# A graph layer on one core: source rows by four partitions and a shuffle, TensorE warmed up, tile 0 ahead of the weights

## The chip, the cores and the metric

The kernel runs on one NeuronCore of a Trainium2 chip. The metric is the device time of one execution in microseconds. The kernel before takes 806.27 us, the median of three runs (795.36 to 811.41).

## What is computed

Every edge takes the normalised rows of its two nodes, puts a linear layer and a ReLU on them, and the message is added to the source node's row of x. In float32, cut to what matters (the layer's own names are put in):

```python
def setup_inputs(seed=0):
    # x: normal, (50000, 512) float32
    # src: 12500 random nodes; dst: 12500 nodes, skewed to the low ones
    # src, dst sorted together by dst
    ...

def _layernorm(x, axis=-1, eps=1e-05):
    m = jnp.mean(x, axis=axis, keepdims=True)
    v = jnp.var(x, axis=axis, keepdims=True)
    return (x - m) / jnp.sqrt(v + eps)

def reference(x, src, dst, L0_gnn_W, L0_gnn_b):
    h = jnp.maximum(_layernorm(x), 0.0)
    # W: (512, 1024), b: (512,)
    x_ij = jnp.concatenate([h[src], h[dst]], axis=1)
    m_ij = jax.nn.relu(x_ij @ W.T + b)
    return x + jax.ops.segment_sum(m_ij, src, num_segments=50000)
```

## The kernel before

The 12500 edges make 98 tiles of 128 edges, one edge a partition (`TILES`). For each tile t:

- POOL gathers the 128 rows of x of the sources and the 128 of the destinations with two indirect DMAs into one of eight buffers of `xg` (`gather`, line 183; a row is 2 KB, a tile 0.52 MB). From tile 8 on it waits on `centred`: ACT must have read the tile that had the buffer.
- DVE takes the statistics of both sides (line 234, once per side), and the scales 1/std by a reciprocal and one Newton step (lines 248 to 261). ACT gives the root (line 409), centres with ReLU (397) and scales (404).
- PE transposes both sides by a product with the identity (line 487, four per side). ACT copies the result rounded to fp32r, `ht_hi` (388), and DVE takes what rounding lost, `ht_lo` (267). The weights are split in the same way, `w_hi` (ACT, 381) and `w_lo` (DVE, 345).
- PE makes 24 products of 128x512 per tile (lines 503 to 505): high by high, high by low, low by high, for each of eight chunks of 128 inputs.
- DVE adds the bias (275), ACT applies the ReLU and rounds, `m_hi` (416), DVE takes the low part, `m_lo` (306).
- Tiles go in pairs. DVE compares the sources of a pair with the tile's own, `same` (288), and counts earlier edges with the same source (290); PE multiplies `same` with the messages (515 to 521), so that each edge holds the sum over its pair for its source; ACT stores these sums into `ring`, 52 tiles deep (425). Every edge but the first of a source in a pair is sent to a spare row behind `out` (`lanes`, 297 and 301).
- POOL adds the sums to `out` by indirect DMA (`add`, 199), two per pair. A pair's adds wait until those of the pair before have landed (`scattered`).

The comparison needs the pair's 256 sources along the free axis on all 128 partitions. ACT loads them into `src_row`, one of two buffers, with a DMA that broadcasts 1 KB to 128 partitions (`load_row`, 373): 128 KB per pair of tiles, 49 times, issued in ACT's odd steps for tiles s + 1 and s + 2.

SP loads indices, the weights in four parts (149; the second and later ones wait until tile 0's rows have arrived) and the bias, and then copies x to `out` with 125 DMAs of 800 KB (163), at most three in flight (`COPY_AHEAD`). The first add waits for all of them. The order of POOL's program is fixed: gathers of tiles 0 to 55, and then, from tile `FIRST_ADD` = 56 on, up to seven pairs of adds for eight gathers; the add of pair 0 stands behind the gather of tile 56. The sums of tile 52 and later reuse `ring` and wait for the adds of tile t - 52.

The engines run their own programs and meet at semaphores. A step s of PE is: transposes of tile s + 1, products of tile s, and in even steps the sums of the pair s - 2. A step of DVE is: statistics of s + 2, bias of s - 1, aggregates of s + 2, `same_source` of s - 1, scales of s + 2, low parts of s + 1, low message and lanes of s - 1. Step s of ACT: high parts of s + 1, message of s - 1, root and centring of s + 2, sums, row load, scaling of s + 2. A wait of DVE on a source row therefore stands ahead of the low parts of tile s + 1, for which PE's next products wait.

## Time and profile before

| | us |
|---|---|
| median of three runs | 806.27 |
| fastest and slowest run | 795.36, 811.41 |
| the profiled execution | 808.76 |
| its span in the profile | 807.0 |
| PE, DVE, ACT, POOL busy | 724.0, 572.9, 475.8, 364.6 |

One execution was profiled. Busy time of PE includes its pipelined overlap, so the record of one 128x512 product is about 400 ns long while the next starts after some 230. PEclk is the granted TensorE clock as a share of 2.4 GHz. Waits are put down to the semaphore that came last. `Lnnn` is a line of the kernel before, as numbered above.

### The profile page before, as it was taken

How to read it: one execution, taken by the hardware profiler on the slowest of the kernel's cores; microseconds unless marked ns; L12 is line 12 of the kernel's file. 1: busy time of each engine (PE TensorE's matmuls, PEld its weight loads, DVE VectorE, ACT ScalarE, POOL GpSimd, SP SyncE). 2: the span in 40 equal slices, each digit the busy share in tenths (PEclk: the TensorE clock that was granted, in tenths of full speed). 3: DMA queues.
4: the chain of work that ended last, by engine and by line, in shares of the span. 5: the costliest groups of instructions: out<-in, count | busy, mean ns of one | idle time of the engine just before them, and what ended most of it. 6: DMA issues, size and time to landing. Idle time of an engine off the chain costs nothing.

```text
span 807.0 us, 13243 instructions
## 1 busy us (share of the span) xinstructions
PE 724.0 (90%) x3430; PEld 588.0 (73%) x3430; DVE 572.9 (71%) x1874; ACT 475.8 (59%) x892; POOL 364.6 (45%) x304
## 2 busy tenths in 40 slices
PE   1499999967799998999999999999999999999950
PEld 1387877756688677877888888888888888888840
DVE  4476867645676686777887887878878788787720
ACT  4465656544566574756765667656576665666610
POOL 6522323222222322223257766666776677644343
PEclk9799999999999999999999999999999999999995
DMA  7999999999999999999558877878787778765664
GB/s 223 404 348 362 354 361 354 342 349 355 353 360 357 341 349 359 358 340 358 185 121 153 142 137 153 154 139 156 147 140 145 146 153 134 154 90 75 84 73 58
DMA packets 42414, 188.95 MB, mean 234 GB/s; under 512 B 7894, under 2 KB 14166, under 8 KB 40384
## 3 DMA queue, kind: packets, MB, share of 16 engines
q0 software_dynamic: 29792, 77.00, 45.5%
q1 hardware_dynamic: 5552, 105.39, 34.1%
q10 hardware_dynamic: 7056, 6.43, 3.9%
q14 instruction: 12, 0.10, 0.0%
q8 instruction: 2, 0.03, 0.0%
HBM read 163.19 MB, written 128.61 MB: 362 GB/s over the span
## 4 chain that ended last, share of the span: by engine, by line
DMA 37%; PE 22%; issue 12%; POOL 12%; DVE 8%; another core or an unknown queue 5%; ACT 3%; ACTq 0%; DVEq 0%; SPq 0%; POOLq 0%
DMA out<-ring,add_i 21%; DMA src_row<-src_rows 14%; POOL out L199 9%; PE z_ps L503 5%; PE z_ps L504 5%; PE z_ps L505 5%; PE ht_ps L487 3%; POOL xg L183 3%; DVE ht_lo L267 1%; DMA ring<-w_t 1%; DVE stats L234 1%; DVE m_lo L306 1%; DVE zb L275 1%; ACT h L397 1%
## 5 line engine op out<-in xcount | busy, mean ns | idle before, releaser
L503 PE MATMUL z_ps<-w_hi,ht_hi 128*128 128x512 f32 x784 | 322.2, 411 | 2.0 <-issue 2.0
L504 PE MATMUL z_ps<-w_lo,ht_hi 128*128 128x512 f32 x784 | 312.7, 399 | 0.0
L505 PE MATMUL z_ps<-w_hi,ht_lo 128*128 128x512 f32 x784 | 312.5, 399 | 0.0
L183 POOL DMA_INDIRECT xg<-x,src_i x98 | 103.6, 1058 | 300.7 <-ACT h L397 285.7
L388 ACT CAST ht_hi<-ht_ps 128x512 fp32r<-128x512 f32 x196 | 106.7, 590 | 223.4 <-PE ht_ps L487 201.2
L199 POOL DMA_INDIRECT out<-ring,add_i x98 | 157.7, 1609 | 103.5 <-DMA out<-ring,add_i 86.2
L505 PEld LDWEIGHTS z_ps<-w_hi,ht_lo 128*128 128x128 f32 x784 | 148.9, 190 | 36.7
L503 PEld LDWEIGHTS z_ps<-w_hi,ht_hi 128*128 128x128 f32 x784 | 150.0, 191 | 34.4 <-issue 2.4
L504 PEld LDWEIGHTS z_ps<-w_lo,ht_hi 128*128 128x128 f32 x784 | 149.8, 191 | 32.2
L234 DVE BATCH_NORM_STATS2 stats<-xg 128x6 f32<-128x512 f32 x196 | 125.6, 682 | 36.7 <-DMA xg<-x,dst_i 32.3
L487 PE MATMUL ht_ps<-identity,h 128*128 128x128 f32 x784 | 109.4, 284 | 41.9 <-ACT h L404 41.8
L404 ACT ACTIVATE h<-h,rstd 128x512 f32<-128x512 f32 x196 | 131.6, 724 | 20.3 <-DVE rstd L261 15.0
L487 PEld LDWEIGHTS ht_ps<-identity,h 128*128 128x128 f32 x784 | 95.6, 147 | 59.7 <-ACT h L404 32.6
L397 ACT ACTIVATE h<-xg,neg_mean 128x512 f32<-128x512 f32 x196 | 130.2, 716 | 0.0
L267 DVE TENSOR_TENSOR ht_lo<-ht_ps,ht_hi 128x512 fp32r<-128x512 f32 x196 | 126.2, 686 | 0.0
L183 POOL DMA_INDIRECT xg<-x,dst_i x98 | 102.0, 1040 | 29.9 <-issue 29.9
L416 ACT ACTIVATE m_hi<-zb 128x512 fp32r<-128x512 f32 x98 | 62.9, 642 | 46.8 <-DVE zb L275 41.4
L275 DVE TENSOR_TENSOR zb<-z_ps,bias_bc 128x512 f32<-128x512 f32 x98 | 67.7, 691 | 15.4 <-PE z_ps L505 12.4
L306 DVE SCALAR_TENSOR_TENSOR m_lo<-zb,m_hi 128x512 fp32r<-128x512 f32 x98 | 66.8, 682 | 0.1
L288 DVE TENSOR_SCALAR same<-src_row,src_f 128x128 fp32r<-128x128 int32 x98 | 32.6, 332 | 48.1 <-DMA src_row<-src_rows 43.5
L248 DVE RECIPROCAL rough<-std 128x2 f32<-128x2 f32 x98 | 16.0, 164 | 69.0 <-ACT std L409 68.4
L425 ACT COPY ring<-agg_ps 128x512 f32 (+1 forms) x98 | 52.2, 588 | 2.1 <-PE agg_ps L518 2.1
(40 smaller groups left out, 404.4 us busy)
## 6 DMA issues: line engine op xcount, KB each, us to landing
out<-x SPq DMA_DIRECT2D x125, 800.0 KB
src_row<-src_rows ACTq DMA_DIRECT2D x49, 128.0 KB
ring<-w_t SPq DMA_DIRECT2D x4, 512.0 KB, 5.2
xg<-x,src_i POOLq DMA_INDIRECT x98
xg<-x,dst_i POOLq DMA_INDIRECT x98
out<-ring,add_i POOLq DMA_INDIRECT x98
out<-x SPq DMA_DIRECT2D x1, 512.0 KB
bias_bc<-bias SPq DMA_DIRECT2D x1, 256.0 KB
```

Of the source, the lines that this page charges most:

```text
L183: nc.gpsimd.indirect_dma_start(out=xg[:, b, s, :], out_offset=None, in_=x, in_offset=bass.IndirectOffsetOnAxis(ap=nodes[:, t:t + 1], axis= ...
L199: nc.gpsimd.indirect_dma_start(out=out, out_offset=bass.IndirectOffsetOnAxis(ap=add_i[:, t:t + 1], axis=0), in_=ring[:, t % RING, :], in_o ...
L234: nc.vector.bn_stats(stats[:, b, s, :], xg[:, m, s, :]).then_inc(stats_done, 1)
L267: nc.vector.tensor_tensor(ht_lo[:, b, s, :], ht_ps[b][s][:, :], ht_hi[:, b, s, :].bitcast(F32), ALU.subtract).then_inc(lo_ready, 1)
L275: nc.vector.tensor_tensor(zb[:, b, :], z_ps[b][:, :], bias_bc[:, :], ALU.add).then_inc(biased, 1)
L388: nc.scalar.copy(ht_hi[:, b, s, :], ht_ps[b][s][:, :]).then_inc(hi_ready, 1)
L397: nc.scalar.activation(h[:, b, s, :], xg[:, m, s, :], ACT.Relu, bias=neg_mean[:, b, s:s + 1]).then_inc(centred, 1)
L404: nc.scalar.activation(h[:, b, s, :], h[:, b, s, :], ACT.Copy, scale=rstd[:, b, s:s + 1]).then_inc(h_ready, 1)
L487: last = nc.tensor.transpose(ht_ps[b][s][:, k * P:(k + 1) * P], h[:, b, s, k * P:(k + 1) * P], identity[:, :])
L503: nc.tensor.matmul(z_ps[b][:, :], hi, w_hi[:, c, :], start=(c == 0), stop=False)
L504: nc.tensor.matmul(z_ps[b][:, :], hi, w_lo[:, c, :], start=False, stop=False)
L505: last = nc.tensor.matmul(z_ps[b][:, :], lo, w_hi[:, c, :], start=False, stop=(c == K - 1))
```

## The change

- `load_row` writes the pair's 256 sources to four partitions only (0, 32, 64, 96) of `row_lanes`, 4 KB, with four buffers instead of two. It goes out three pairs ahead. POOL clears `row_lanes` once at the start, and ACT's first four loads wait for that. For each even tile DVE spreads each of the four partitions over its 32 with a `stream_shuffle` into `src_row`, now a single buffer, and waits for its own shuffle (`row_spread`).
- `zb` has one buffer instead of two.
- PE runs 60 transposes of the identity, in a loop of 15 times four, before tile 0's.
- SP issues two weight loads, not one, before it waits for tile 0's rows.
- ACT and DVE make the high and low parts of tile 0 right behind its scaling, ahead of the weights' third and later chunks; DVE takes tile 1's statistics later.
- POOL sets its two bounds registers behind the clearing of `row_lanes`; they are registers in both versions.

```diff
@@ -30,9 +30,12 @@
     PAIRS = TILES // 2
     W_LOADS = 4
     W_FIRST = 2
+    WARM = 60
     XS = 8
     RING = 52
     FIRST_ADD = 56
+    ROWS = 4
+    LANES = 32
     COPY_RUNS = 16
     COPY_ROWS = COPY_RUNS * 25
     COPIES = N // COPY_ROWS
@@ -81,14 +84,15 @@
         h = sb("h", [P, 2, SIDES, D], F32)
         ht_hi = sb("ht_hi", [P, 2, SIDES, KD * P], F32R)
         ht_lo = sb("ht_lo", [P, 2, SIDES, KD * P], F32R)
-        src_row = sb("src_row", [P, 2, 2 * P], I32)
+        row_lanes = sb("row_lanes", [P, ROWS, 2 * P], I32)
+        src_row = sb("src_row", [P, 2 * P], I32)
 
 
         same = sb("same", [P, 3, P], F32R)
         found = sb("found", [P, 2 * P], F32)
         count = sb("count", [P, 2], F32)
         move = sb("move", [P, 2], F32)
-        zb = sb("zb", [P, 2, OUT], F32)
+        zb = sb("zb", [P, OUT], F32)
         m_hi = sb("m_hi", [P, 2, OUT], F32R)
         m_lo = sb("m_lo", [P, 2, OUT], F32R)
 
@@ -108,7 +112,9 @@
         eps_made = sem("eps_made")
         spare_made = sem("spare_made")
         x_arrived = [sem(f"x_arrived{b}") for b in range(XS)]
-        row_arrived = [sem(f"row_arrived{b}") for b in range(2)]
+        lanes_made = sem("lanes_made")
+        row_arrived = [sem(f"row_arrived{b}") for b in range(ROWS)]
+        row_spread = sem("row_spread")
         scattered = sem("scattered")
         src_cast = sem("src_cast")
         w_hi_ready = sem("w_hi_ready")
@@ -142,7 +148,7 @@
             sp.dma_start(src_i[:, :], src_cols).then_inc(src_loaded, 16)
             w_chunks = w_t.rearrange("(k p) o -> p k o", p=P)
             for n in range(W_LOADS):
-                if n == 1:
+                if n == 2:
 
                     sp.wait_ge(x_arrived[0], 16 * SIDES)
                 ks = slice(n * K // W_LOADS, (n + 1) * K // W_LOADS)
@@ -170,8 +176,6 @@
 
         @block.gpsimd
         def _(pool):
-            last_node = pool.to_reg(N - 1)
-            last_row = pool.to_reg(N + 2 * P - 1)
 
             def gather(t):
                 b = t % XS
@@ -201,6 +205,9 @@
                         in_=ring[:, t % RING, :], in_offset=None, bounds_check=last_row,
                         compute_op=ALU.add).then_inc(scattered, 16)
 
+            nc.gpsimd.memset(row_lanes[:, :, :], 0).then_inc(lanes_made, 1)
+            last_node = pool.to_reg(N - 1)
+            last_row = pool.to_reg(N + 2 * P - 1)
             nc.gpsimd.iota(spare_i[:, :], pattern=[[P, 2]], base=N, channel_multiplier=1).then_inc(spare_made, 1)
             nc.gpsimd.memset(eps[:, :], EPS).then_inc(eps_made, 1)
             nc.gpsimd.memset(identity[:, :], 0.0).then_inc(consts, 1)
@@ -272,18 +279,21 @@
                 if not isinstance(t, int):
 
                     dve.wait_ge(stats_done, SIDES * (t + 4))
-                nc.vector.tensor_tensor(zb[:, b, :], z_ps[b][:, :], bias_bc[:, :], ALU.add).then_inc(biased, 1)
+                nc.vector.tensor_tensor(zb[:, :], z_ps[b][:, :], bias_bc[:, :], ALU.add).then_inc(biased, 1)
 
             def same_source(t, m):
 
-                b, row_slot = m % 2, m // 2 % 2
-
-                dve.wait_ge(row_arrived[row_slot], 4 * (t - m) + 16 * (m // 4) + 16)
+                b = m % 2
+                if b == 0:
+                    dve.wait_ge(row_arrived[m // 2], 2 * (t - m) + 16)
+                    nc.vector.stream_shuffle(src_row[:, :], row_lanes[:, m // 2, :], [0] * LANES
+                                             ).then_inc(row_spread, 2)
+                    dve.wait_ge(row_spread, t + 2)
                 if not (isinstance(t, int) and t < 2):
                     dve.wait_ge(agg_done, t - 1)
 
                 width = (b + 1) * P
-                row = src_row[:, row_slot, 0:width]
+                row = src_row[:, 0:width]
                 mine = src_f[:, bass.ds(t, 1)]
                 nc.vector.tensor_scalar(same[:, b:2 * b + 1, :].rearrange("p a j -> p (a j)"), row, mine, None,
                                         ALU.is_equal).then_inc(same_ready, 1)
@@ -303,7 +313,7 @@
 
             def message_low(t, b):
                 dve.wait_ge(mhi_ready, t + 1)
-                nc.vector.scalar_tensor_tensor(out=m_lo[:, b, :], in0=zb[:, b, :], scalar=0.0,
+                nc.vector.scalar_tensor_tensor(out=m_lo[:, b, :], in0=zb[:, :], scalar=0.0,
                                                in1=m_hi[:, b, :].bitcast(F32), op0=ALU.max, op1=ALU.subtract
                                                ).then_inc(mlo_ready, 1)
 
@@ -349,10 +359,10 @@
             statistics(0, 0)
             aggregate(0, 0)
             scales(0, 0)
+            low_parts(0, 0)
+            w_low_parts(W_FIRST, KD)
             statistics(1, 1)
             aggregate(1, 1)
-            w_low_parts(W_FIRST, KD)
-            low_parts(0, 0)
             w_low_parts(KD, K)
             scales(1, 1)
             dve.wait_ge(bias_loaded, 16)
@@ -370,8 +380,8 @@
         def _(act):
             def load_row(t, slot):
 
-                act.dma_start(src_row[:, slot, :],
-                              src_rows[0:1, bass.ds(t * P, 2 * P)].to_broadcast([P, 2 * P])
+                act.dma_start(row_lanes[0::LANES, slot, :],
+                              src_rows[0:1, bass.ds(t * P, 2 * P)].to_broadcast([P // LANES, 2 * P])
                               ).then_inc(row_arrived[slot], 16)
 
             def w_high_parts(first, end):
@@ -413,7 +423,7 @@
                 act.wait_ge(biased, t + 1)
                 if not (isinstance(t, int) and t < 2):
                     act.wait_ge(agg_done, t - 1)
-                nc.scalar.activation(m_hi[:, b, :], zb[:, b, :], ACT.Relu).then_inc(mhi_ready, 1)
+                nc.scalar.activation(m_hi[:, b, :], zb[:, :], ACT.Relu).then_inc(mhi_ready, 1)
 
             def store_sums(t, again):
 
@@ -440,15 +450,16 @@
                     centre(s + 2, (m + 2) % XS)
                 if b and has(-3):
                     store_sums(s - 3, again)
-                if b and has(-2) and has(2):
+                if b and has(-3) and has(2 * ROWS - 2):
 
                     act.wait_ge(counted, s - 1)
-                    load_row(s + 1, (m + 1) // 2 % 2)
+                    load_row(s + 2 * ROWS - 3, (m - 3) % XS // 2)
                 if has(2):
                     divide(s + 2, b)
 
-            load_row(0, 0)
-            load_row(2, 1)
+            act.wait_ge(lanes_made, 1)
+            for pair in range(ROWS):
+                load_row(2 * pair, pair)
             act.wait_ge(eps_made, 1)
 
             nc.scalar.activation(warm[:, :], eps[:, :], ACT.Sqrt)
@@ -456,8 +467,8 @@
             deviation(0, 0)
             centre(0, 0)
             divide(0, 0)
+            high_parts(0, 0)
             w_high_parts(W_FIRST, KD)
-            high_parts(0, 0)
             w_high_parts(KD, K)
             deviation(1, 1)
             centre(1, 1)
@@ -533,6 +544,9 @@
                     sums(s - 2)
 
             pe.wait_ge(consts, 4)
+            with pe.Fori(0, WARM // 4):
+                for k in range(KD):
+                    nc.tensor.transpose(ht_ps[1][0][:, k * P:(k + 1) * P], identity[:, :], identity[:, :])
             transposes(0, 0)
             products(0, 0)
             transposes(1, 1)
```

DVE in the main loop, where the source row is compared (the operations of one even tile). Before:

```order
68 L240 BN_AGGR mean_var<-stats 128x2 x2
69 L242 TENSOR_SCALAR neg_mean<-mean_var 128x2
70 L281 REGISTER_ALU
71 L283 REGISTER_ALU
72 L288 ISA
73 L288 TENSOR_SCALAR same<-src_row,src_f 128x128
74 L290 SCALAR_TENSOR_TENSOR found,count<-src_row,src_f,earlier 128x128
```

Now:

```order
69 L247 BN_AGGR mean_var<-stats 128x2 x2
70 L249 TENSOR_SCALAR neg_mean<-mean_var 128x2
71 L288 ISA
72 L289 STREAM_SHUFFLE src_row<-row_lanes 128x256
73 L291 REGISTER_ALU
74 L293 REGISTER_ALU
75 L298 ISA
76 L298 TENSOR_SCALAR same<-src_row,src_f 128x128
77 L300 SCALAR_TENSOR_TENSOR found,count<-src_row,src_f,earlier 128x128
```

The shuffle stands ahead of `same`, and with it everything of the step behind that; row 71 is part of the wait for the load, 75 of the one for the sums.

ACT at the start, from its first instruction on. Before:

```order
1 L373 DMA src_row<-src_rows 128x256 x2
2 L454 ACT_TABLE_LOAD
3 L454 ACTIVATE warm<-eps 128x1
4 L381 CAST w_hi<-ring 128x512 x2
5 L409 ACTIVATE std<-mean_var,eps 128x2
6 L397 ACTIVATE h<-xg,neg_mean 128x512 x2
7 L404 ACTIVATE h<-h,rstd 128x512 x2
8 L381 CAST w_hi<-ring 128x512 x2
9 L388 CAST ht_hi<-ht_ps 128x512 x2
10 L381 CAST w_hi<-ring 128x512 x4
```

Now:

```order
1 L383 DMA row_lanes<-src_rows 4x256 x4
2 L465 ACT_TABLE_LOAD
3 L465 ACTIVATE warm<-eps 128x1
4 L391 CAST w_hi<-ring 128x512 x2
5 L419 ACTIVATE std<-mean_var,eps 128x2
6 L407 ACTIVATE h<-xg,neg_mean 128x512 x2
7 L414 ACTIVATE h<-h,rstd 128x512 x2
8 L398 CAST ht_hi<-ht_ps 128x512 x2
9 L391 CAST w_hi<-ring 128x512 x6
```

Four small row loads stand where two large ones did, and the two high parts of tile 0 (the cast of `ht_ps`) have moved ahead of six of the eight casts of the weights.

PE at the start. Before:

```order
0 L479 UNCONDITIONAL_BRANCH
1 L487 MATMUL ht_ps<-identity,h 128x128 x8
2 L503 MATMUL z_ps<-w_hi,ht_hi 128x512
```

Now:

```order
0 L490 UNCONDITIONAL_BRANCH
1 L547 UNCONDITIONAL_BRANCH
2 L549 MATMUL ht_ps<-identity 128x128 x4
3 L547 REGISTER_ALU
4 L547 COMPARE_AND_BRANCH
5 L498 MATMUL ht_ps<-identity,h 128x128 x8
6 L514 MATMUL z_ps<-w_hi,ht_hi 128x512
```

Rows 1 to 4 are the loop of the identity's transposes, ahead of those of tile 0.

## Rows read from the trace of the kernel before

**Rows 1.** The page: traffic in 40 slices of 20.2 us, and its HBM line
```profile
GB/s 223 404 348 362 354 361 354 342 349 355 353 360 357 341 349 359 358 340 358 185 121 153 142 137 153 154 139 156 147 140 145 146 153 134 154 90 75 84 73 58
...
HBM read 163.19 MB, written 128.61 MB: 362 GB/s over the span
```
**Rows 2.** The view by stretches: start:end, length, busy us (instructions) of each engine, PEclk, DMA share, GB/s
```profile
core 0: us, PE busy (x) PEld busy (x) DVE busy (x) ACT busy (x) POOL busy (x), PEclk, DMA share, GB/s
40.00:140.00 100.00, 96.42 (x448) 77.81 (x448) 71.47 (x243) 61.45 (x115) 26.77 (x27) 0.96 1.00 359
140.00:215.00 75.00, 60.82 (x276) 48.27 (x275) 42.82 (x139) 35.32 (x65) 14.38 (x14) 0.95 0.98 350
215.00:345.00 130.00, 122.63 (x575) 99.08 (x573) 96.40 (x323) 81.63 (x153) 35.01 (x34) 0.96 0.98 352
...
389.00:411.00 22.00, 21.89 (x107) 17.56 (x106) 19.37 (x63) 15.60 (x29) 7.80 (x8) 1.00 0.40 118
411.00:704.00 293.00, 293.00 (x1434) 240.86 (x1433) 238.65 (x776) 193.64 (x369) 203.15 (x153) 1.00 0.78 146
```
**Rows 3.** The waits: us in total, times, longest; whole span, then 140 to 215 us
```profile
DVE same L288 <- DMA src_row<-src_rows: 43.5, 11, 6.3
...
DVE stats L234 <- DMA xg<-x,dst_i: 32.3, 9, 6.4
...
DVE stats L234 <- DMA xg<-x,dst_i: 27.1, 6, 6.4
```
**Rows 4.** The view by stretches of line 234, the statistics, two instructions a tile
```profile
0.00:150.00 150.00, 21.80 (x34) 0.94 0.97 345
```
**Rows 5.** The timeline: start us, us, instruction [idle before <- what ended it]; POOL's gathers, DVE's statistics
```profile
91.71 1.01 POOL L183 DMA_INDIRECT xg<-x,src_i  x1 [5.10 <-ACT h L397]
...
150.71 1.29 DVE L234 BATCH_NORM_STATS2 stats<-xg 128x6 f32<-128x512 f32 x2 [3.49 <-DMA xg<-x,dst_i]
...
327.25 1.01 POOL L183 DMA_INDIRECT xg<-x,src_i  x1 [5.52 <-ACT h L397]
...
384.24 1.29 DVE L234 BATCH_NORM_STATS2 stats<-xg 128x6 f32<-128x512 f32 x2 [2.21 <-DMA xg<-x,dst_i]
```
**Rows 6.** The DMA queues from 57 to 389 us: packets, MB, share of 16 engines
```profile
q1 hardware_dynamic: 3613, 92.58, 72.7%
q0 software_dynamic: 6724, 22.03, 21.7%
q10 hardware_dynamic: 2904, 2.65, 4.0%
```
**Rows 7.** The timeline of POOL: the first add, the last tile's gather, the last pair
```profile
411.15 1.63 POOL L199 DMA_INDIRECT out<-ring,add_i  x1 [0.30 <-issue]
...
703.06 1.09 POOL L183 DMA_INDIRECT xg<-x,src_i  x1 [1.75 <-ACT h L397]
...
796.25 1.56 POOL L199 DMA_INDIRECT out<-ring,add_i  x1 [4.09 <-DMA out<-ring,add_i]
```
**Rows 8.** The timeline of DVE in the steady stretch
```profile
563.79 0.36 DVE L288 TENSOR_SCALAR same<-src_row,src_f 128x256 fp32r<-128x256 int32 x1
...
572.60 0.17 DVE L248 RECIPROCAL rough<-std 128x2 f32<-128x2 f32 x1 [1.53 <-ACT std L409]
...
573.49 1.29 DVE L267 TENSOR_TENSOR ht_lo<-ht_ps,ht_hi 128x512 fp32r<-128x512 f32 x2
```
**Rows 9.** The timeline of PE, the products that follow those low parts
```profile
577.40 0.48 PE L503 MATMUL z_ps<-w_hi,ht_hi 128*128 128x512 f32 x1
```
**Rows 10.** The view by stretches of PE: busy us (matmuls), PEclk
```profile
31.00:44.00 13.00, 5.87 (x18) 0.50 1.07 410
```
**Rows 11.** The timeline of PE: transposes of tiles 0, 2 and 3
```profile
14.84 1.51 PE L487 MATMUL ht_ps<-identity,h 128*128 128x128 f32 x6 [14.84 <-ACT h L404]
...
38.13 1.97 PE L487 MATMUL ht_ps<-identity,h 128*128 128x128 f32 x8 [10.39 <-ACT h L404]
...
47.47 1.04 PE L487 MATMUL ht_ps<-identity,h 128*128 128x128 f32 x8
```

## The prediction

> **What bounds the kernel now.** I read the page first: in its GB/s slices the traffic stands at 340 to 400 after the first and falls from 358 to 185 in the twentieth, about 387 us [rows 1]. So there are two stretches: one in which the copy of x to `out` fills the DMA engines, and one without it. Cutting the span there [rows 2], the DMA share is 0.98 to 1.00 before and 0.40 behind 389 us, while PE goes from gaps to 100% busy. A tile has 8 transposes, 24 products and 3 of a pair's 6 sums, 35 matmuls; so 448 of them in 40 to 140 us are 12.8 tiles, 7.8 us each; from 140 to 215 it is 9.5 us, from 215 to 345 7.9 us, from 411 to 704 7.15. The last is PE's own pace. Against it the first three stretches lost 12.8 x 0.65 = 8, 7.9 x 2.35 = 19 and 16.4 x 0.75 = 12 us, 39 in all.
>
> What ended DVE's idle time [rows 3]: the row of sources for 43.5 us in 11 waits, the gathered rows of x for 32.3 us in 9, of which 27.1 fall between 140 and 215 us, where no row wait stands.
>
> The gathers are hardly better off than the rows. 34 statistics had run by 150 us [rows 4], so the one at 150.71, which waited 3.49 us, is tile 17's; its gather, the 18th pair on POOL, went out at 91.71 [rows 5]: 59 us from issue to use, with only eight buffers. The same count finds tile 45, gathered at 327.25 and waited for at 384.24 [rows 5]: 57 us again, at the end of a stretch in which the trace names only rows as the culprit. The DMA engines from 57 to 389 us [rows 6] are busy 72.7% with the copy, 21.7% with gathers, 4.0% with row loads: 98% full. **The first stretch is bound by DMA work, and the row waits mostly hide gather waits behind them.**
>
> How the second half hangs on the first: POOL issues its gathers and its adds from one program. The first add stands behind the gather of tile 56, which waits for ACT to free the buffer of tile 48; it goes out at 411.15, about 22 us after the copy ended [rows 7]. Then seven pairs of adds go with eight gathers, and these wait for ACT, which keeps PE's pace: the last tile's gather at 703.06 waited 1.75 us for it. 13 pairs follow in the 104 us to the span's end at 807, the last at 796.25 after 4.09 us of waiting for the pair before [rows 7]. So the end is the pace of the tiles up to the last gather, plus 104 us that nothing in the change touches. A tile chain that comes out of the copy earlier by d ends the span earlier by d, until the copy itself holds the first add.
>
> **The change part by part.**
>
> Row loads. Each wrote 128 KB, now 4 KB. Those from 57 to 389 us took 4.0% of 332 us = 13.3 us of all 16 engines [rows 6]; nearly all of it goes. The engines are full, so copy and gathers both move up by it: copy end 389 to about 376, gathers of tile 45 from 384 to about 371. This is the largest term: -13.3.
>
> The row waits. Loads now go out three pairs ahead instead of one, so the 43.5 us of waiting go. I give them nothing beyond the term above. Before 140 us what they gave back is taken by tile 17, whose gather came at 150.7 whatever the chain had done before. Later the gathers stay the limit at tile 45. What is late next is therefore the gather: I expect DVE's wait on xg to grow from 32 to about 45 us.
>
> The Trainium skill, "DMA: Bandwidth & Descriptors", Queues, rings and completion order, says that each DMA engine goes round the queue rows that hold work and drains one packet of a row before it turns to the next. By that rule gathers that are always queued get their turns however early the chain wants them; the 59 and 57 us of [rows 5] agree. Without such turns most of the 39 us lost up to 345 us could come back, which is rival A.
>
> The shuffle. One more DVE operation for a pair of tiles, 49 in all, and a wait of DVE on its own semaphore. The trace has no shuffle. The nearest row by shape is the comparison over 128x256, 0.36 us [rows 8]; it cannot be below nothing, since it is an added operation of an engine that works in order, and as the far end I take the two low parts over 128x512, 1.29 us [rows 8]. I take 0.4 and 0.1 for the wait: 25 us of DVE work. Behind it on DVE stand `same`, the scales and the low parts, for which PE waits. In the steady stretch DVE idles 1.53 us before L248 in just that step, waiting for ACT, and the low parts are done at 574.78, while the products that read them start at 577.40 [rows 8, 9]. So up to 1.53 + 2.6 = 4.1 us are hidden: cost 0. The Trainium skill, "VectorE: DVE Perf Modes", The perf-mode tier table, has the shuffle at about 2400 ns for 2048 elements a partition in its only mode; an estimate from that page is 0.3 us here, and the sum would be the same.
>
> The loads of the start. Two of the four weight loads now go before tile 0 has arrived, 0.5 MB earlier into engines that are not yet full: at some 350 GB/s [rows 2] about 1.4 us less before the copy; tile 0's gather shares the engines with them and comes up to 1 us later, and the loads behind it too. Net -0.5, between -1.5 and +2.
>
> Tile 0 ahead of the weights, and the 60 turns. From 31 to 44 us, after PE had stood idle for 10.39 us, its granted clock was 0.50, that is 1.2 GHz; in the gapless stretch it is 1.00, 2.4 GHz [rows 2, 10, 11]. Eight transposes take 1.97 us at the one and 1.04 at the other [rows 11]. So the 60 turns take 8 to 15 us from about 3 us on and end between 11 and 18; tile 0's transposes started at 14.84 [rows 11]. If the clock is up by then, its 24 products take about half their time, 5 to 6 us less. That is between 3 us lost and 6 gained by tile 0, and worth 0 at the end: tile 17 still waits for its gather. The larger memset on POOL is done while the first gather waits for src_i; the bounds are set once either way; `zb` as one buffer is rewritten only after DVE itself has read it. Four row loads on ACT's queue instead of two go while ACT waits for the weights. Cost 0.
>
> Sum: 808.8 (the profiled execution, span 807.0) - 13.3 - 0.5 = 795.0. The median shown is 2.5 lower, 806.3, so 792.5; I say 792. A measurement of this kernel, whose runs spread from 795 to 811, can tell about 2% (16 us) from no change, so my forecast lies just inside.
>
> **Rivals.**
>
> A. The chain runs at PE's pace through the copy. For it: outside 140 to 215 us only 5 of the 32.3 us lie [rows 3], so gathers were ahead of the tiles in most of the copy. Against it: they had fallen back to 57 us of latency and a wait at tile 45. Then the copy holds the first add. The gathers took 21.7% of 332 us for 22.03 MB, 42 tiles of 0.52 MB [rows 6], so 1.7 us a tile; four more before the copy's end (tile 56's is the last that may go) make 7, so it ends at 389 - 13.3 - 0.5 + 7 = 382 and the first add goes at about 384 instead of 411: -27. Adds that no longer wait for the tiles, may gain 5 more (the first 36 pairs took 8.1 us each from 411.15 to 703.06, the last 12 some 7.8): 806.3 - 27 - 5 = 774.
>
> B. The 13 us come back as slower packets: if memory, not the engines, is full, the copy's packets stretch as soon as the rows are gone. For it: the GB/s are flat at 350 to 360 whatever the mix [rows 1, 2]. Against it: the page's HBM total is 362 GB/s over the whole span, the copy-free half included [rows 1], so during the copy it is far higher and no such ceiling is seen at 360. Result 806.3 - 1 to -4: 804.
>
> C. Slower: the shuffle is far dearer than its neighbours. From 4.1 us on, each further microsecond delays the low parts in each of the 25 pairs behind the copy: at 5.5 us it is 1.4 x 25 = 35, so 792 + 35 = 827. The shuffle decides from there; below 4.1 us it costs nothing. For it: the trace has no shuffle. Against it: that is over ten times its nearest row.
>
> D. The warm-up turns do nothing, because the clock has fallen again when tile 0 comes. It changes nothing at the end, as above, and shares the forecast's number.
>
> **How the numbers follow.** Forecast (with D) 0.43, its own range 784 to 799; A 0.29; B 0.22; C 0.06. Range: down to A's number with a little of the spread of the runs, 771, and up past B's to 806. Faster by over 2% (below 790): nearly all of A (0.27) and 0.19 of the forecast, whose centre is 2 us off the line: 0.46. Slower by over 2%: 0.05 from C. Within: 0.49.
>
> **What the profile after would show.** Right: the row queue's share falls from 3.9% to near nothing; no wait of `same` on a DMA; DVE waits on xg for 40 us or more; the GB/s fall one slice earlier; the first add near 397, the last gather near 690; PE gapless after the copy; the shuffle at 0.3 to 0.5 us. A wait on xg under 20 us and a first add near 384 say A. The copy's end unmoved at 389 says B. New idle time of PE in the steady stretch says C. The step most likely wrong is the one that gives the row waits nothing beyond their DMA work.

## The result, and the profile after

On the chip the changed kernel took 760.62 us (median of 4 runs, 760.39 to 761.98), the kernel before 808.84 (4 runs, 795.36 to 821.38): a ratio of 0.950, with an interval of 0.939 to 0.961. The ratios of this document leave out the profiled execution and every run over 1.5% above the fastest of its kernel's others, while medians and ranges are of all runs, so the gain by the ratio is 40 us (800.8 to 760.9) and not the 48 between the medians. The profiled executions have spans of 807.0 and 759.1 us, 47.9 apart; the one before was itself 8 us over those 800.8, so what is read from the pair of traces below is somewhat more than the change gives. The forecast was 792, with 771 as the lower end of its range, so it was wrong by more than its range allowed. The mechanism of rival A is what happened, and it went further than the 774 us given for it.

The page after, traffic in 40 slices of 19.0 us and the HBM line, as in [rows 1]:

```profile
GB/s 276 360 381 365 364 351 374 349 374 362 370 364 359 372 369 351 372 363 344 314 117 142 159 133 147 152 151 133 167 129 152 143 135 143 148 65 78 63 82 55
HBM read 156.96 MB, written 128.61 MB: 376 GB/s over the span
```

The fall comes behind the twentieth slice, at 380 us; before, it came in the twentieth of the longer slices. In the copy the slices stand mostly at 350 to 375, where they stood at 340 to 360: more is moved per second, although the row loads are gone. The view by stretches, cut as in [rows 2] (length, busy us and instructions of PE, PEld, DVE, ACT and POOL, PEclk, DMA share, GB/s):

```profile
40.00:140.00 100.00, 100.00 (x483) 82.37 (x482) 83.29 (x282) 65.52 (x126) 28.26 (x29) 0.98 1.00 364
140.00:215.00 75.00, 75.00 (x371) 61.70 (x370) 62.65 (x211) 49.29 (x95) 21.74 (x22) 1.00 1.00 363
215.00:345.00 130.00, 130.00 (x636) 106.88 (x635) 107.89 (x364) 85.98 (x166) 36.63 (x36) 1.00 1.01 365
```

PE has no gap left in the copy. Its 1490 matmuls from 40 to 345 us are 42.6 tiles at 7.16 us, its own pace; before there were 1299, 37.1 tiles. That is 5.5 tiles more, 39 us at PE's pace: all that the prediction counted as lost. DVE's and POOL's waits:

```profile
DVE stats L241 <- DMA xg<-x,dst_i: 11.0, 4, 6.4
POOL xg L187 <- ACT h L407: 223.0, 50, 6.3
POOL out L203 <- DMA out<-ring,add_i: 82.4, 42, 4.1
```

The two DMA waits of DVE in [rows 3], 43.5 and 32.3 us, have become one of 11.0. It did not grow, as the forecast said, to 40 or more. The queues from 57 to 389 us, as in [rows 6]:

```profile
q1 hardware_dynamic: 3571, 91.04, 71.2%
q0 software_dynamic: 8019, 25.87, 26.9%
q10 hardware_dynamic: 184, 0.09, 0.1%
```

The row queue fell from 4.0% to 0.1%, as it should. But it is the gathers that grew, from 21.7% to 26.9%. The copy's share is lower only because the copy now ends 9.5 us inside this window; up to 360 us it is 73.2% before and 73.4% after. POOL's timeline at the places of [rows 7] (the first add, the last tile's gather, the last pair of adds):

```profile
380.89 1.63 POOL L203 DMA_INDIRECT out<-ring,add_i  x1 [17.95 <-issue]
655.16 1.08 POOL L187 DMA_INDIRECT xg<-x,src_i  x1 [0.31 <-ACT h L407]
748.32 1.56 POOL L203 DMA_INDIRECT out<-ring,add_i  x1 [3.91 <-DMA out<-ring,add_i]
```

The first add goes at 380.89 us instead of 411.15, and POOL stood 17.95 us ahead of it on "issue", until the copy had ended (its last packets in the trace end at 379.5). So the copy holds it, not the tiles. The 36 pairs up to the last gather then take 274.3 us instead of 291.9, 7.62 us a pair instead of 8.11, since the tiles are so far ahead that POOL hardly waits for ACT (0.31 us at the last gather, 1.75 before). The rest to the span's end is 103.9 us, before 104.

| part of the span | before | after | difference |
|---|---|---|---|
| start to the first add | 411.2 | 380.9 | -30.3 |
| first add to the last gather | 291.9 | 274.3 | -17.6 |
| last gather to the end | 103.9 | 103.9 | 0 |

The two new pieces of work, as groups of the view by line:

```profile
L289 DVE STREAM_SHUFFLE src_row<-row_lanes 128x256 int32<-128x256 int32 x49 | 22.1, 450 | 0.2
L549 PE MATMUL ht_ps<-identity 128*128 128x128 f32 x60 | 9.6, 341 | 3.2 <-POOL earlier L218 3.2
```

The shuffle takes 0.45 us and the 60 turns 9.6 us.

### The profile page after: what moved, and what is told of

The parts are those of the page before. It is cut to its first block, busy times and chain, and to the rows that moved or that the text cites. A ratio compares the mean times of both kernels' runs of the same rounds, so it can differ in the third digit from the quotient of the medians.

```text
span 759.1 us, 13504 instructions
## 1 busy us (share of the span) xinstructions
PE 717.7 (95%) x3490; PEld 589.7 (78%) x3490; DVE 590.6 (78%) x1972; ACT 470.0 (62%) x892; POOL 365.3 (48%) x305
## 4 chain that ended last, share of the span: by engine, by line
PE 78%; DMA 9%; issue 5%; POOL 5%; DVE 1%; ACT 0%; SPq 0%; POOLq 0%; DVEq 0%; ACTq 0%
PE z_ps L514 20%; PE z_ps L515 20%; PE z_ps L516 20%; PE ht_ps L498 10%; DMA out<-ring,add_i 6%; POOL out L203 4%; DMA xg<-x,dst_i 3%; POOL xg L187 2%; PE agg_ps L526 1%; PE agg_ps L532 1%; PE agg_ps L527 1%; PE agg_ps L528 1%; PE agg_ps L531 1%; PE agg_ps L529 1%; DMA src_i<-src_cols 0%
## 5 line engine op out<-in xcount | busy, mean ns | idle before, releaser
L514 PEld LDWEIGHTS z_ps<-w_hi,ht_hi 128*128 128x128 f32 x784 | 147.9, 189 | 34.0 <-issue 1.5
L515 PEld LDWEIGHTS z_ps<-w_lo,ht_hi 128*128 128x128 f32 x784 | 148.1, 189 | 31.8
L498 PE MATMUL ht_ps<-identity,h 128*128 128x128 f32 x784 | 103.7, 276 | 7.4 <-ACT h L414 7.4
L498 PEld LDWEIGHTS ht_ps<-identity,h 128*128 128x128 f32 x784 | 92.6, 142 | 21.8 <-ACT h L414 9.2
L300 DVE SCALAR_TENSOR_TENSOR found<-src_row,src_f,earlier 128x128 f32<-128x128 int32 x98 | 40.4, 412 | 0.0
```

What stands on the lines that cost most here:

```text
L498: last = nc.tensor.transpose(ht_ps[b][s][:, k * P:(k + 1) * P], h[:, b, s, k * P:(k + 1) * P], identity[:, :])
L514: nc.tensor.matmul(z_ps[b][:, :], hi, w_hi[:, c, :], start=(c == 0), stop=False)
L515: nc.tensor.matmul(z_ps[b][:, :], hi, w_lo[:, c, :], start=False, stop=False)
```

## The experiments

The changed kernel took 760.6 us in the result and 767.9 and 770.3 us beside the third and fourth group below, so comparisons are made within a group, whose kernels shared a chip and the runs of the kernel before. Where a group had no control of its own, that is said.

**First group: which part, and is it the waits or the loads?** The kernel before took 798.87 us here (7 runs, 791.52 to 803.1). Three theories stood against each other: the gain comes from the row waits that go, from the row loads' work on the DMA engines that goes, or from the start.

The edits of the rows alone, `rows_only`: the changed kernel without the loop of 60 turns, with `if n == 1:` again and the old order of the weights' parts.

> The row edits alone (four partitions, shuffle, four buffers, three pairs ahead, one zb), start as in the kernel before. Theory R (the row loads were all of it): 760 to 768 us, first add near 382, DVE waits on gathers under 20 us. Theory S (the start edits are needed, because gathers that go out earlier at the start keep every DMA engine level): 780 to 795 us, with waits on gathers of 40 us or more.

Measured: 762.92 us (762.22 to 763.85), ratio 0.958 (0.951 to 0.965).

The edits of the start alone, `start_only`: the kernel before with those three.

> The start edits alone (60 turns, tile 0 ahead of the weights, two weight loads first), rows as before. Theory R: 800 to 812 us, row waits of some 40 us as before. Theory S: 775 to 795 us.

Measured: 806.31 us (785.21 to 814.78), ratio 1.013 (1.000 to 1.025), no gain. But its four runs spread over 30 us, and the profiled one, 785.21, lies below every run of the kernel before, so this kernel alone does not settle the start; the last pair of this section does. The gain of `rows_only` is as large as that of the whole change.

Wide loads three pairs ahead, `wide_ahead`: the row waits are taken away, the loads' work is kept.

```diff
-                    nc.vector.stream_shuffle(src_row[:, :], row_lanes[:, m // 2, :], [0] * LANES
-                                             ).then_inc(row_spread, 2)
-                row = src_row[:, 0:width]
+                row = row_lanes[:, m // 2, 0:width]
-                act.dma_start(row_lanes[0::LANES, slot, :],
-                              src_rows[0:1, bass.ds(t * P, 2 * P)].to_broadcast([P // LANES, 2 * P])
+                act.dma_start(row_lanes[:, slot, :],
+                              src_rows[0:1, bass.ds(t * P, 2 * P)].to_broadcast([P, 2 * P])
```

> The changed kernel, but each row load again writes all 128 partitions (128 KB), into four buffers and three pairs ahead, and there is no shuffle. Theory W (the waits of DVE on rows were the loss, since a late load stopped the chain): 765 to 778 us, copy ending 13 us later than in the changed kernel, first add near 394. Theory D (the load's packets in the DMA engines were the loss: they made one engine fall behind with the gathers): 795 to 810 us, waits on rows near 0 but waits on gathers of 60 us or more.

Measured: 794.08 us (784.83 to 804.15), ratio 0.990 (0.979 to 1.000). Its waits of DVE hold no row:

```profile
DVE stats L241 <- DMA xg<-x,dst_i: 59.6, 19, 7.3
```

The row waits are gone, the waits on gathers are 59.6 us instead of 32.3, and by the ratio 8 us came of it, with an interval from 0 to 17. The time lies in neither range that was expected, 1 us below the one for the loads' work. A gain of that size is close to what the prediction said of the row waits by themselves.

Narrow loads one pair ahead, `narrow_near`: the loads' work is taken away, the distance is the old one.

```diff
-    ROWS = 4
+    ROWS = 2
-                if b and has(-3) and has(2 * ROWS - 2):
+                if b and has(-2) and has(2):
-                    load_row(s + 2 * ROWS - 3, (m - 3) % XS // 2)
+                    load_row(s + 1, (m + 1) // 2 % 2)
```

> The changed kernel with loads of 4 KB, but only two buffers, one pair ahead as before. Theory W: a load on four engines with one packet each still queues behind the copy's packets; if it lands within about 11 us of its issue there are no waits and the time is 760 to 765, if it takes 15 us or more waits of 10 to 40 us come back and the time is 770 to 790. Theory D: 760 to 765 us whatever the distance.

Measured: 761.65 us (760.42 to 763.09), ratio 0.957 (0.950 to 0.964), the same as `rows_only`. Four buffers and three pairs of distance add nothing once the load is small; what counts is the load of 128 packets from one place against that of four. But by what? The row queue had only 4% of the engines. The queues of the kernel before and of `wide_ahead` from 57 to 360 us, a stretch in which the copy runs in every kernel (in `add52_ahead4`, below, to 359.0 us):

```profile
q1 hardware_dynamic: 3304, 84.95, 73.2%
q0 software_dynamic: 6061, 19.85, 21.5%
q10 hardware_dynamic: 2678, 2.44, 4.1%
```
```profile
q1 hardware_dynamic: 3244, 83.31, 71.7%
q0 software_dynamic: 6263, 20.54, 22.5%
q10 hardware_dynamic: 2618, 2.38, 4.3%
xg<-x,src_i POOLq DMA_INDIRECT x36, 17.8
xg<-x,dst_i POOLq DMA_INDIRECT x37, 59.8
```

And the changed kernel in the same stretch:

```profile
q1 hardware_dynamic: 3357, 85.92, 73.4%
q0 software_dynamic: 7262, 23.81, 26.5%
q10 hardware_dynamic: 168, 0.09, 0.1%
xg<-x,src_i POOLq DMA_INDIRECT x42, 14.7
xg<-x,dst_i POOLq DMA_INDIRECT x42, 31.8
```

The shares sum to 98.8 and 98.5% with wide loads and to 100.0% without. What the gathers won over the kernel before, 5.0% of 303 us, is the 4.0% of the rows and engine time that had been idle. The second half of a gather lands 31.8 us after its issue, against 59.8 in `wide_ahead`.

**Second group: what in a row load costs?** The kernel before took 809.66 us (7 runs, 797.1 to 818.75). Each kernel is the changed one with 28 more loads during the copy, four ahead of ACT's first step (from 38.6 us on in `extra_few`) and one in each turn where ACT issues a row load. They go to two slots of `ring` (50, 51) that are free until then, and nothing reads them. The theories: it is the number of packets, the bytes, or that all 128 packets read one and the same 1 KB.

```diff
+            def load_extra(j):
+                act.dma_start(ring[:, 50 + j // 2, j % 2 * 256:j % 2 * 256 + 256],
+                              bias[0:1, 0:256].to_broadcast([P, 256])).then_inc(extra_in[j], 16)
...
+                    if not isinstance(s, int) and not again:
+                        d = (m - 3) % XS
+                        act.wait_ge(extra_in[d // 2], 2 * (s - d) + 10)
+                        load_extra(d // 2)
```

That is `extra_same`, 128 packets of 1 KB from one place.

> The changed kernel plus 28 loads during the copy that nobody uses, each the same 1 KB of HBM to 128 partitions (8 packets for each of the 16 engines). Theory T (only the DMA time that the packets take): 28 x 0.64 us = 18 us of the copy at most, 765 to 779 us. Theory P (each such packet takes a turn from the gathers) and theory H (16 engines read one place of HBM at once, and one falls behind): 780 to 800 us, DVE waits on gathers of 30 us or more.

`extra_rows` reads `x[128 * j:128 * j + 128, 0:256]` instead, 128 packets of 1 KB from 128 places.

> The same 28 unused loads with the same 128 packets of 1 KB, but each packet reads another row of x. Theory T: 765 to 779 us. Theory P: as extra_same, 780 to 800. Theory H: 761 to 779, with waits on gathers under 15 us.

`extra_big` has the same 128 KB as 32 packets of 4 KB, from rows of x.

> 28 unused loads of the same 128 KB in 32 packets of 4 KB. Theory P (packets count): a quarter of extra_rows' cost over the changed kernel's 761. Theory T (bytes and DMA time count): about the same cost as extra_rows. Theory H: 761 to 775.

`extra_few` has only 16 of the packets of `extra_rows`.

> 28 unused loads of 16 packets of 1 KB (16 KB, one packet an engine). All theories that count packets, bytes or time: an eighth of extra_rows' cost, 761 to 765 us. If the number of loads itself counts: as slow as extra_rows.

| kernel | packets, KB each | median us (lowest to highest) | ratio | profiled us | DVE on xg, us |
|---|---|---|---|---|---|
| extra_same | 128, 1, one place | 824.63 (808.77 to 867.25) | 1.029 (1.006 to 1.052) | 808.77 | 49.7 |
| extra_rows | 128, 1 | 780.97 (777.19 to 797.94) | 0.971 (0.954 to 0.988) | 782.75 | 16.1 |
| extra_big | 32, 4 | 776.5 (775.24 to 796.03) | 0.968 (0.952 to 0.985) | 776.55 | 8.0 |
| extra_few | 16, 1 | 778.57 (770.6 to 793.21) | none was given | 773.4 | 1.0 |

The one that reads one place costs 44 us more than its twin by the medians and 26 by the profiled executions, for the same bytes in the same number of packets. It was also slower than the 780 to 800 expected of it. By its number alone `extra_rows`, 781, lies on the edge of what the theory of packets gave it; what speaks against that theory is the distance between the twins, which it puts at nothing. The three that read different places differ little. This group had no control; against the 767.9 us that the changed kernel took on this chip in the next one, they stand 9 to 13 us higher by the medians. The medians do not say that 16 packets cost as much as 128: of the four runs of `extra_few` two (770.6 and 773.4) lie below every run of the other two kernels, two (783.75 and 793.21) do not, and it has no ratio. Nor need all of the 9 to 13 us be the loads'. In all four traces of this group ACT stands idle for 16.5 to 17.2 us at tile 0's cast, which `after_again` below does not show, and it ends ahead of the first unused load. ACT in `extra_few`:

```profile
30.54 1.07 ACT L403 CAST ht_hi<-ht_ps 128x512 fp32r<-128x512 f32 x2 [17.21 <-remote]
...
38.63 0.93 ACTq L389 DMA_DIRECT2D ring<-x  x2
```

The row queue (q10) of `extra_same` and of `extra_rows` from 57 to 380 us:

```profile
q10 hardware_dynamic: 3312, 2.95, 8.0%
```
```profile
q10 hardware_dynamic: 3499, 3.11, 3.4%
```

8.0% of 323 us on 16 engines are 413 us for 3312 packets, 0.125 us each; 3.4% are 176 us, 0.050 each. In the kernel before a packet took 4.1% x 303 x 16 / 2678 = 0.074 us.

**Third group: the place alone.** The kernel before took 797.88 us (7 runs, 794.72 to 814.76). First the control, the changed kernel itself, `after_again`.

> The changed kernel as it is, a control on this chip: 760 to 763 us, and the measure for the other three runs. If the startup stall of some 17 us that the runs with unused loads showed is the chip's and not theirs, it may show here too, without moving the time by over 2 us.

Measured: 767.9 us (767.09 to 768.97), ratio 0.964 (0.961 to 0.967), above the 760 to 763 that were expected.

`rep_rows` is the kernel before with one thing changed: the list of sources lies in HBM 128 times, and each partition reads its own copy. Packets, bytes, buffers and distance stay.

```diff
-                              src_rows[0:1, bass.ds(t * P, 2 * P)].to_broadcast([P, 2 * P])
+                              src_rows[:, bass.ds(t * P, 2 * P)]
-        "src_rows": np.ascontiguousarray(src_pad.reshape(1, -1)),
+        "src_rows": np.ascontiguousarray(np.broadcast_to(src_pad.reshape(1, -1), (128, tiles * 128))),
```

> The kernel BEFORE, with one edit: the list of sources lies 128 times in HBM and each partition's load reads its own copy, so the 128 packets of 1 KB stay and no two read the same place. No shuffle, two buffers, one pair ahead. Theory H (128 reads of one place of HBM were the loss): 768 to 785 us, as extra_rows; waits on gathers under 15 us, and of the row waits at most 25 us are left. Theories P and T (packets, their bytes, or the waits): 795 to 812 us, as before.

Measured: 777.38 us (775.18 to 778.64), ratio 0.976 (0.972 to 0.980). Two thirds of the whole gain of this group, 19 of 28 us by the ratios, come of reading other places. Its waits, and its queues from 57 to 360 us:

```profile
DVE same L288 <- DMA src_row<-src_rows: 55.5, 17, 6.2
DVE stats L234 <- DMA xg<-x,dst_i: 9.4, 4, 4.8
```
```profile
q1 hardware_dynamic: 3270, 83.72, 71.9%
q0 software_dynamic: 6787, 22.22, 24.7%
q10 hardware_dynamic: 2829, 2.57, 3.2%
xg<-x,dst_i POOLq DMA_INDIRECT x39, 44.5
```

A packet takes 0.055 us instead of 0.074, the shares sum to 99.8%, and the gathers have 24.7% instead of 21.5. The row waits, of which at most 25 us were expected to be left, are longer than the 43.5 us before, and the kernel is 19 us faster all the same: it goes with the gathers, whose waits fell from 32.3 to 9.4 us. The copy ended no earlier (391.5 us, before 389.3); the first add went at 392.94 instead of 411.15, right behind the copy, and the 36 pairs up to the last gather took 280.1 us instead of 291.9 (against the one profiled execution of the kernel before, 808.76 us).

Two runs asked whether more can be had. `add52` sets `FIRST_ADD = 52`, so that the first add stands behind an earlier gather; `add52_ahead4` sets `COPY_AHEAD = 4` as well, one more piece of the copy in flight.

> The changed kernel with FIRST_ADD 52 instead of 56. If the end is the copy's end plus 49 pairs of adds, one behind the other (378 us), then four gathers fewer ahead of the first add, 1.7 us of the DMA engines each, bring it and the end forward by 5 to 7 us: 753 to 757. If the chain of tiles ended the span, or the DMA engines were not the copy's limit: 760 to 763.

> add52 with four copies in flight instead of three. Engines that the copy left idle are filled, and the gathers have some 25 us in hand: first add 5 us earlier or more than in add52, 745 to 754 us, down to the floor of PE's chain at about 742. If three already keep every engine busy: as add52, or slower by waits on gathers.

Measured: `add52` 765.83 us (764.23 to 768.41), ratio 0.963 (0.959 to 0.967): 2 us under the control, with intervals that overlap, where 5 to 7 were expected. Its first add went at 383.17 instead of 387.6, 4 us earlier, and little of it reached the end. `add52_ahead4` 883.06 us (877.66 to 887.12), ratio 1.111 (1.103 to 1.119), a clear loss, against an expected 745 to 754. Its waits of DVE, and its queues from 57 to 360 us:

```profile
DVE stats L241 <- DMA xg<-x,dst_i: 162.3, 29, 7.5
```
```profile
q1 hardware_dynamic: 3543, 90.32, 82.5%
q0 software_dynamic: 4443, 14.57, 16.9%
xg<-x,dst_i POOLq DMA_INDIRECT x25, 85.1
```

The copy ended early, at 359.0 us, and the gathers paid for it: 16.9% of the engines where `add52` has 24.6%, 25 tiles gathered instead of 38, and a first add at 466.2.

**Fourth group: how many engines at one place?** The kernel before took 806.88 us (12 runs, 794.33 to 822.99). `rep16_block` is the kernel before with 16 copies of the list, of which neighbouring partitions share one, eight to a copy; `rep8_mod` has 8 copies, and partition p reads copy p mod 8.

```diff
-                              src_rows[0:1, bass.ds(t * P, 2 * P)].to_broadcast([P, 2 * P])
+                              src_rows[:, bass.ds(t * P, 2 * P)].unsqueeze(1).to_broadcast([16, 8, 2 * P])
```

```diff
-                              src_rows[0:1, bass.ds(t * P, 2 * P)].to_broadcast([P, 2 * P])
+                              src_rows[:, bass.ds(t * P, 2 * P)].unsqueeze(0).to_broadcast([16, 8, 2 * P])
```

> The kernel before with 16 copies of the source list in HBM; partition p reads copy p // 8, so that the packets of one DMA engine (eight neighbouring partitions, if the split is by blocks) all read one place, and no two engines share one. If many engines at one place were the loss: 770 to 782 us, as rep_rows. If it was an engine's repeated reads of one place: 790 to 810, as before.

> The kernel before with 8 copies; partition p reads copy p % 8, so that each engine's eight packets read eight places and all 16 engines read the same eight. If many engines at one place were the loss: 785 to 810 us, somewhat better than before where they are not in step. If it was an engine's repeated reads: 770 to 782.

Measured: 776.68 us (776.37 to 778.97), ratio 0.974 (0.969 to 0.980), and 789.68 us (784.51 to 796.66), ratio 0.987 (0.978 to 0.996). Eight partitions in a row that read one copy are as good as 128 copies (0.976 in the third group). Where sixteen partitions spread over all of them read one copy, only half of that gain is left, 10 of 21 us by the ratios. The queues of `rep16_block` and of `rep8_mod` from 57 to 360 us:

```profile
q1 hardware_dynamic: 3281, 84.33, 72.3%
q0 software_dynamic: 6839, 22.40, 24.1%
q10 hardware_dynamic: 3015, 2.75, 3.6%
```
```profile
q1 hardware_dynamic: 3309, 84.64, 74.1%
q0 software_dynamic: 6325, 20.73, 23.0%
q10 hardware_dynamic: 2862, 2.61, 3.0%
```

The slower kernel has the shorter row packets (0.051 us against 0.058), and no idle share; what it has less of is gathers. So neither the row packets' own time nor idle engine time tells which kernel is slow. The first adds go at 391.93 and 391.47 us, and the difference comes up to the last gather, at 671.08 and 682.29. A place may then be read eight times at no cost that shows. Two explanations are left, and no run here separates them: how many different DMA engines read one place, or merely how many reads it gets (eight or sixteen). The first is how I read it, but both expectations assume that an engine has eight neighbouring partitions, and no view here shows the engines apart; 16 copies with partition p at copy p mod 16 would decide.

The ranges go the same way. The kernels without a load that 128 partitions read from one place mostly repeat within 2 to 6 us (the changed kernel, `rows_only`, `narrow_near`, `rep_rows`, `rep16_block`), those with one spread over 12 to 58 us; but `rep8_mod` spreads over 12 and the unused loads from different places over some 20.

The two repeats separate the start from the rows once more, with six runs each.

> The row edits alone, beside the changed kernel on one chip. The prediction gave the start edits nothing at the end: the two within 2 us of each other. If the earlier weights and the warmed PE carry through to the copy's end: this one 4 us slower or more.

> The changed kernel, control for the other three: 760 to 768 us, by the chip.

Measured: `rows_only_2` 768.85 us (765.77 to 772.09), ratio 0.963 (0.959 to 0.968); `after_2` 770.28 us (768.28 to 770.83), ratio 0.965 (0.961 to 0.969). No gain of the start is seen, and the two are within the 2 us that were expected.

## Why the prediction was wrong

**What bounds the kernel**: right in its first half. The first stretch is bound by DMA work, and the row waits by themselves hide gather waits behind them. `wide_ahead` is that sentence as a kernel: no row wait, 59.6 us on xg, and 8 us won (0 to 17).

**The row loads, -13.3: this step failed.** It took their cost to be their packets' time, 4.0% of the engines, and it let "copy and gathers both move up by it". Both were wrong.

First, the size. A load that 128 packets read from one place costs the others more than its own time. `rep_rows` gives back 19 us without taking one packet away, and the loads and waits that are left are worth 9.5 us more (777.4 to 767.9); `extra_rows` puts about as much packet work in again and stands 13 us above the control by the medians. So 13.3 us was if anything too much for the packets' own work, and two thirds of the effect did not stand in the row that I multiplied.

Second, the exchange. The two do not move up together. From 57 to 360 us the copy got 73.2% before and 73.4% after; all that came free went to the gathers, 5.0% of 303 us = 15 us. A tile's gather needs far less engine time, 1.7 us by [rows 6], than the 7.15 us that the chain takes for the tile. So 15 us of engines went with 42.3 tiles instead of 36.6 (1480 matmuls instead of 1282, 35 a tile, in the row shown below), and 5.7 tiles are 41 us of the chain. That closes the 39 us. The copy's end moved by 10 us only (389.3 to 379.5), since it had more gathers beside it. The stretch from 57 to 360 us, first of the kernel before, then of the changed one:

```profile
57.00:360.00 303.00, 276.50 (x1282) 222.13 (x1280) 207.67 (x691) 178.34 (x333) 76.28 (x74) 0.97 0.99 354
```
```profile
57.00:360.00 303.00, 303.00 (x1480) 249.05 (x1480) 251.53 (x849) 200.31 (x383) 85.34 (x84) 1.00 1.00 363
```

The copy-bound stretch moved 3% more a second, and PE did 15% more. The 3% are within what one kernel's traces differ by: in `after_again` and `after_2` it moved 356 and 357 GB/s, and PE did as much as here.

That the freed time went to the gathers is seen in the shares; that eight buffers turn it into 41 us of chain is worked out from them and was not tried by itself.

**The gathers taken as the limit whatever the chain does**, the ground for "the gathers stay the limit at tile 45" and for nothing beyond -13.3 there: wrong. Eight buffers at 7.15 us a tile allow 57 us from a gather's issue to the tile's use, and 59 and 57 were measured before [rows 5]. I read this as a limit of the queue; the runs fit a threshold better. In the changed kernel the second half lands after 31.8 us, well under it, and the wait is all but gone; in `add52` it lands after 44.7 us, and DVE still waits 21.4 us, so the threshold is not sharp. The Trainium skill, "DMA: Bandwidth & Descriptors", Queues, rings and completion order, has every engine take one packet of each queue row with work in turn. I had taken from it that the gathers' share is given. The runs do not bear that out: from 57 to 360 us it was 16.9% with one more piece of the copy in flight, 21.5 before and 26.5 in the changed kernel.

**Rival A** had this mechanism and nearly the size of its first term: copy end at 382 (measured 379.5), first add at 384 (380.9), -27 (-30.3, from an execution before that was 8 us over the mean behind the ratio). Its second term, 5 us for adds that no longer wait for the tiles, measured 17.6. I had compared 8.1 us for the first 36 pairs with 7.8 for the last 12; they ran at 7.62. With 5 us in that term it came to 774 where 761 was measured; it had a chance of 0.29 against the forecast's 0.43.

**Rival B** (packets stretch, 804): no. The copy's packets took 73.2% x 4848 / 3304 = 1.074 us before and 1.060 after, so they did not stretch; in `after_again` they took 1.084, and the gain is there all the same. **Rival C**: no, the shuffle is 0.45 us against 0.4 predicted, and hidden (PE keeps 7.16 us a tile through the copy).

**The start**: right. The 60 turns took 9.6 us (8 to 15 predicted), and neither `start_only` against the kernel before nor `after_2` against `rows_only_2` shows a gain. That the start has room is seen in `after_2`, where PE stood idle for some 17 us behind tile 0's transposes, for a reason that I did not find (ACT's cast of them waited, and its releaser is given as "remote"; the trace of the kernel before has such a wait of 9.5 us, that of `rows_only_2` one of 8.5, that of the changed kernel none). PE from 12 to 24 us in the changed kernel, then from 12 to 24 and 24 to 30 in `after_2`:

```profile
12.00:24.00 12.00, 9.43 (x48) 1.00 1.05 382
```
```profile
12.00:24.00 12.00, 1.98 (x16) 0.66 1.01 378
24.00:30.00 6.00, 0.00 (x0) 0.50 1.03 373
```

The granted clock is 0.50, 1.2 GHz, after the idle time, and 1.00, 2.4 GHz, where PE had work. Yet `after_2` is only 1.4 us above `rows_only_2`, with intervals of the ratio that overlap: the copy holds the first add, and a tile chain that starts late is hidden by it.

**The last 104 us** were untouched, as said. **The expected marks**: the first add near 397 and the last gather near 690 were missed (381, 655); "a wait on xg under 20 us and a first add near 384 say A" was the mark that came true, and the step named as the likeliest to be wrong stood next to the one that was: the waits at nothing of their own are within the interval of `wide_ahead` and agree with `narrow_near`, the loads at 13.3 us were wrong.

**Open**: what in the memory or the engines makes reads of one place dear. The packets' own extra time is (0.074 - 0.055) x 2829 / 16 = 3 us in `rep_rows`, against 19 us won. From the kernel before to `rep_rows` the gathers gained 3.2% of the engines: 0.9 from the rows, 1.0 from idle time and 1.3 from the copy. But `rep8_mod` is slow without idle time and with short row packets, so neither idle time nor long row packets can be the whole cause, and which engine waits for which was not tried.

## What to carry to other kernels

A load that broadcasts one short row to 128 partitions is not small because its queue is: look at what the other queues get, and read one place from a few partitions and spread the row on an engine that has time, or store copies of it. Where a prefetch lands at about its number of buffers times the pace of the consumer, a small change of the load can decide between starved and free. Do not share freed DMA time out evenly: here it went to that prefetch, 15 us of engines beside 41 us of chain. Ask of each stage separately what holds it: here one cause paid twice, at the first add and in the pace of the adds behind it.

## What the runs showed of the hardware

- 28 loads of 128 KB whose 128 packets read one 1 KB cost 26 to 44 us more than 28 loads with the same packets from different places; their packets took 0.125 us against 0.050. Sixteen copies, each read by eight neighbouring partitions, were as good as 128 copies; eight copies, each read by sixteen partitions spread over all, won half of that.
- How many pieces of a large copy are in flight sets how the engines are shared: with four instead of three, the copy went from about 74 to 82.5% and the gathers from about 25 to 16.9% (`add52_ahead4`; `add52` had 74.8 and 24.6%), which cost 117 us.
- A stream shuffle over 128x256 int32 took 450 ns.
- The changed kernel took 760.6 us in the result, 767.9 on a second occasion and 770.3 on a third, with 363, 356 and 357 GB/s from 57 to 360 us. The last two were on two different chips; which chip the first was on is not on record, so that the chip makes the difference is likely and not shown.
